# Expert routing one unit earlier on VectorE and ScalarE, in a four-stage attention and mixture-of-experts kernel

## What is computed

```
x = x + tanh(gx[0]) * attention0(layernorm(x), ctx)       # one head of width 128
x = x + tanh(gf[0]) * experts0(layernorm(x))              # 16 experts of width 64, top 4, and a shared one
x = x + tanh(gx[1]) * attention1(layernorm(x), ctx)       # 16 heads of width 8
x = x + tanh(gf[1]) * experts1(layernorm(x))              # 8 experts of width 128, top 2
```

## Time and profile before

| | us |
|---|---|
| median of 3 runs | 331.32 |
| lowest and highest run | 330.4, 331.4 |
| the profiled execution | 328.63 |
| its span, first to last instruction | 326.7 |

### The profile page before, as it was taken

The page is one execution under the profiler, slowest core; times in us unless marked ns, Lnnn a source line. Parts: engine busy times, 40 slices in busy tenths (PEclk is TensorE's granted clock), DMA queues, the critical chain, the costliest instruction groups (busy, mean ns, idle before and its releaser), DMA issues.

```text
span 326.7 us, 5592 instructions
## 1 busy us (share of the span) xinstructions
PE 289.0 (88%) x1470; PEld 216.5 (66%) x1470; DVE 243.6 (75%) x714; ACT 163.1 (50%) x435; POOL 103.4 (32%) x160
## 2 busy tenths in 40 slices
PE   6699699989899599589888888988978999999995
PEld 5588476666566376268778778778856667676662
DVE  2887989689579976546697787877968877868572
ACT  1587542432422232676887887889742242332321
POOL 6374200101191510564549539629110010100000
PEclk9999999999979899959999999999999999999999
DMA  6900175586791420000000000000032242151550
GB/s 220 325 25 0 48 225 156 159 231 192 220 246 48 140 98 32 0 2 0 0 4 0 2 1 0 0 0 3 0 108 99 55 155 104 52 178 33 182 174 32
DMA packets 16408, 28.98 MB, mean 89 GB/s; under 512 B 2661, under 2 KB 4659, under 8 KB 16179
## 3 DMA queue, kind: packets, MB, share of 16 engines
q1 hardware_dynamic: 14312, 27.71, 27.6%
q10 hardware_dynamic: 2072, 0.99, 1.2%
HBM read 24.29 MB, written 1.25 MB: 78 GB/s over the span
## 4 chain that ended last, share of the span: by engine, by line
PE 59%; DVE 15%; ACT 9%; DMA 7%; issue 6%; SPq 4%; DVEq 1%; ACTq 0%
PE bank L564 23%; PE Ybank L586 14%; PE bank L757 4%; DMA CR<-comb_rows 3%; ACT PX L1025 3%; DVE cmx L1410 2%; DMA comb_rows<-ct 2%; PE Tb L503 2%; SPq L326 2%; DMA X<-in_x 2%; DVE recT L1426 2%; ACT QS L1013 1%; PE bank L741 1%; PE bank L602 1%; DVE st L1117 1%
## 5 line engine op out<-in xcount | busy, mean ns | idle before, releaser
L908 ACT ACTIVATE sg<-bank 128x512 f32<-128x512 f32 x64 | 38.0, 595 | 73.7 <-PE bank L564 62.0
L1277 DVE TENSOR_TENSOR hb<-sg,CR 128x512 f32<-128x512 f32 x64 | 44.6, 696 | 17.0 <-issue 7.0
L355 POOL TENSOR_TENSOR rstd<-ve,mhalf 128x4 f32<-128x4 f32 x11 | 11.1, 1011 | 131.5 <-DVE ve L1124 131.5
L1270 DVE TENSOR_TENSOR sg<-sg,bank 128x512 f32<-128x512 f32 x64 | 43.5, 680 | 4.5 <-ACT sg L908 2.2
L1410 DVE TENSOR_REDUCE cmx<-bank 128x4 f32<-128x308 f32 x64 | 28.3, 471 | 17.4 <-PE bank L730 17.2
L564 PE MATMUL bank<-xh,WBH 128*128 128x512 f32 x68 | 35.6, 524 | 5.4 <-DVE sg L1270 4.0
L372 POOL TENSOR_TENSOR KS<-kr,CB 128x1232 fp32r<-128x1232 f32 x16 | 36.2, 2268 | 11.3 <-PE bank L730 11.3
L564 PE MATMUL bank<-xh,UPH 128*128 128x512 f32 x64 | 36.2, 565 | 0.0
L586 PE MATMUL Ybank<-hb,W2T 128*128 128x512 f32 x64 | 33.8, 610 | 1.6 <-DVE hb L1277 1.6
L586 PE MATMUL Ybank<-hb,downw 128*128 128x512 f32 x64 | 32.9, 598 | 0.1
L1025 ACT ACTIVATE PX<-bank,cmx 128x77 f32<-128x77 f32 x128 | 29.3, 354 | 0.0
(11 more groups left out here) (184 smaller groups left out, 598.5 us busy)
## 6 DMA issues: line engine op xcount, KB each, us to landing
CR<-comb_rows SPq DMA_DIRECT2D x64, 128.0 KB, 3.2
CR<-comb_rows SPq DMA_DIRECT2D x32, 256.0 KB, 3.4
VX<-in_vs_seed SPq DMA_DIRECT2D x4, 320.0 KB, 5.5
kr<-kh SPq DMA_DIRECT2D x8, 154.0 KB, 3.2
kr<-kl SPq DMA_DIRECT2D x8, 154.0 KB, 3.3
w13raw<-in_w SPq DMA_DIRECT2D x1, 1088.0 KB, 11.4
X<-in_x SPq DMA_DIRECT2D x4, 256.0 KB, 6.5
upraw<-in_up SPq DMA_DIRECT2D x4, 256.0 KB, 4.5
```

The costliest lines, as they stand in the source:

```text
L355: nc.gpsimd.tensor_tensor(rstd[:], ve[:], mhalf[:], ALU.pow).then_inc(rstd_rdy, 1)
L908: A(sg[:, k % 2, :], Gb[k % 2][:], ACT.Silu).then_inc(m.s_done, 1)
L1270: V.tensor_tensor(sg[:, k % 2, :], sg[:, k % 2, :], Ub[k % 2][:], ALU.mult).then_inc(m.t2, 1)
L1277: V.tensor_tensor(hb[:, k % 2, :], sg[:, k % 2, :], CR[:, k % RING, :], ALU.mult).then_inc(m.h_done, 1)
```

## The change

VectorE's `route_pick` goes from unit 4 to unit 3 and `route_weights` from unit 5 to unit 4; ScalarE's `m_route_tanh` goes from unit 5 to unit 4, and `m_route_copy` from unit 6 to unit 5. In both stages, for all six boundaries. TensorE's and the SP queue's programs are as before.

```diff
@@ ScalarE, m_body
                     if nxt is not None and nxt[1] is not None and k == 3:
                         m_route_act(nxt[1], nxt[2])
+                    if nxt is not None and nxt[1] is not None and k == m.units - 4:
+                        m_route_tanh(nxt[1], nxt[2])
                     if nxt is not None and nxt[1] is not None and k == m.units - 3:
-                        m_route_tanh(nxt[1], nxt[2])
-                    if nxt is not None and nxt[1] is not None and k == m.units - 2:
                         m_route_copy(nxt[1], nxt[2])
@@ VectorE, m_body
                     if nm is not None and k == 3:
                         route_vals(nm, ng)
                         route_top(nm, ng)
+                        route_pick(nm, ng)
                     if nm is not None and k == 4:
-                        route_pick(nm, ng)
-                    if nm is not None and k == 5:
                         route_weights(nm, ng)
                     if stats_of is not None and k == m.units - 2:
                         norm_stats(n + 1, stats_of)
```

## The result

The changed kernel takes 339.12 us (median of 4 runs, 337.77 to 339.48), the kernel before 331.36 beside it (median of 4). The ratio of the runs is 1.0257, with a 95% interval of 1.0207 to 1.0307: slower, by 8.5 us. I had forecast slower, by 4.45 us. Applied to 331.4 us the ratio gives 339.9 us, just above the range that I gave (332.0 to 339.6). The place was right, the size was not. Ratios here are of fast runs alone, and medians of all runs, so a ratio need not be the quotient of two medians; where I set a measurement against a range in microseconds I give both.

The account below looks back on a forecast made before the run. TensorE, busy 88% of the span, was taken as the bound. Six boundary losses summed to +6.15 us, less 1.7 for the clock: +4.45 on the 331.32 us median, giving 335.8 us, range 332.0 to 339.6.

Parts of the forecast that it names:

- the first loss of part 2: Group 1: TensorE, free at 78.92, starts the next group's unit 0 at 79.62, losing 0.70 us.
- "nothing lost" of part 1: VectorE's earlier pick: gating of unit 4 ends at 74.13, before TensorE's 74.30, so nothing is lost.
- the clock's -1.7: Low-clock stretch at 91.1 to 94.5 us goes as TensorE's 1.52 us wait shrinks: -1.7 us, bounds -1.7 to 0.
- The mechanism of part 2: ScalarE's earlier copy waits for TensorE's turn and holds SiLU 6, gating and TensorE: 1.45 us lost at one boundary.
- VectorE's own delay: VectorE's gating of unit 6 starts at 78.88 instead of 77.43, which carries 1.45 us to TensorE's unit 2.
- The boundaries that take up the loss: First stage: TensorE's waits ahead of the logits absorb loss, leaving +0.6 (group 0 to 1) and +0.1 (1 to 2).
- rival B: Late SiLU 6 costs the same, but the clock falls as before: 337.5 us, chance 0.22.
- Rival C: TensorE's new waits lower the clock further, two low stretches of 1.7 us each: 340.9 us, chance 0.1.
- Rival F: The row comes out sooner, removing TensorE's waits of 0.84 and 1.52 us: 329.0 us, chance 0.05.

Follow-up runs that it names:

- copy only: Kernel before with only ScalarE's copy of the turned weights moved one unit earlier, VectorE's program and the tanh unchanged: 336.17 us, ratio 1.0132.
- splits moved: GpSimd's four up-weight splits put behind its first two key expansions: on the kernel before 328.28 us, on the changed kernel 337.44 us.
- both GpSimd moves: Kernel before with GpSimd's splits behind its first two key expansions and the expansions behind VectorE's normalization, routing unchanged: 323.52 us, ratio 0.9840.
- VectorE only: Kernel before with pick, weights and tanh one unit earlier, ScalarE's copy left where it was: 330.99 us, ratio 1.0022.

## Why the prediction was right in place and too small

**ScalarE's wait: right in place, too small.** Three steps of the sum failed: the first loss of part 2, "nothing lost" of part 1, and the clock's -1.7. The mechanism of part 2 is shown by undoing it (no loss in D) and by doing it alone (all of D's loss). The term "TensorE is free at 78.92 and starts at 79.62: 0.70 us lost" was mis-sized. In TensorE's timelines the second product of unit 0 follows the turn's start by 1.20 us before (78.98 less 77.78), by 2.17 after (82.69 less 80.52): 0.97 lost. I had set the six products behind a wait at their usual 1.39. The chain of waits of the changed kernel shows what they take, in D:

```profile
287.82 0.12 PE Tb L616
288.00 0.36 issue
288.56 0.56 ACT sg L908
289.14 0.70 DVE sg L1270
...
292.71 1.65 PE bank L564 x6
294.36 0.86 PE Ybank L586 x2
295.22 1.51 PE bank L564 x6
```

1.65 us: a group of products that starts from a wait has its first weight load open ahead of it, while in the steady run the load goes under the down product. The rows of weight loads agree; the changed kernel first, then before, where the down product runs from 77.89 to 78.91:

```profile
82.35 0.19 PEld L564 LDWEIGHTS bank<-xh,WBH 128*128 128x128 f32 x1 [1.53 <-DVE sg L1270]
```

```profile
78.32 0.19 PEld L564 LDWEIGHTS bank<-xh,WBH 128*128 128x128 f32 x1 [0.24 <-DVE sg L1270]
```

(The Trainium skill, "TensorE: Matmul & The Clock Gate", Step-by-step: what each phase is for, says that weight loads are pulled ahead of running products; the load at 78.32, inside the down product, agrees.) So the first wait of a boundary costs 0.26 more than its idle time. At the last boundary this stays (forecast 0.8, measured 1.21); where VectorE's own delay carries the loss on, as at D's first (1.67 for 1.55), it is swallowed by the next wait.

Part of the rest of D's excess is ScalarE's start. Before, the copy began 0.39 us behind the turn's start at D's second and third boundary (280.62 to 281.01 at the second); after, 0.70 (287.66 to 288.36) and 0.48. All six versions with the copy at unit 5 show 0.69 or 0.70 and 0.47 or 0.48 at the same places, the others 0.39 or 0.40, so it belongs to the order and not to chance. Why the copy starts later there is open.

**VectorE's part: "Nothing lost" was wrong.** I set the end of a gating against the times of TensorE's products in the chain, 74.30 and 76.55. But the timeline of the kernel before has unit 7's first product start at 75.98:

```profile
75.98 0.80 PE L564 MATMUL bank<-xh,WBH 128*128 128x512 f32 x1
```

It overlaps the down product, and its gate must be there by then, 0.6 us sooner than I took it. So what I counted as 0.1 us in group 1 was 0.7: from the logits (72.12) to the copy of the row (80.83) 8.71 us instead of 8.00 (70.08 to 78.08). In group 0 it was 0.3 (9.15 for 8.83). In D the turn came at most 0.1 us later behind the logits than before, as I had said.

**Group 2: the cost of a moved step was taken from another place.** I priced pick and weights by group 1's durations and wrote that they shift nothing. In group 2 the splits of GpSimd run beside the small operations between SBUF tiles, and these take 0.3 to 1.1 us longer than elsewhere. Before, the pick stood behind gating 4, where the splits had ended. Now gating 4 starts 2.7 us later behind the logits (5.54 us, from 95.66 to 101.20, against 2.88) and TensorE waits 2.06 us. Of the 2.7, 1.6 are the pick with its slow copy. The other 1.0 is the two unmoved operations, and copy only has it too (3.90): it comes from where the splits fall against the logits, and why they fell otherwise there is open. I had seen such a clash and used it for the normalization alone. The changed kernel with the splits moved shows it: 8.69 us instead of 10.74. (The Trainium skill, "Advanced Engine Details and Errata", Mode Summary, has VectorE's second SBUF port shared with GpSimd; the trace agrees in that gatings, with one input from PSUM, stay at 0.68 beside a split (at 95.86 in the changed kernel), and goes beyond that section in that a product of two SBUF tiles takes 2.33 us beside a key expansion.)

**The boundaries that take up the loss: mostly right.** Group 1 to 2 gained 0.8 us where I had said 1.6, mostly for the later turn; the wait ahead of the logits and the low clock behind it went as I had said. Group 0 to 1 lost 0.96 for 0.6, by the later turn too.

**The clock's -1.7: there in its stretch, not in the whole.** With the routing of before, the run with the splits moved waited 1.06 us ahead of these logits and the one with both GpSimd moves 0.74, and neither had low clock at 91 us; "VectorE only" waited 1.09 us ahead of the logits at 66.73 and had it there. So the wait of 1.52 us and the low stretch are the profiled execution's, and that the change removed them is not shown. Over the whole kernel nothing came back: the mean granted clock is 0.979 in both profiled executions, and 0.977 to 0.979 in the changed kernel's four runs. That is rival B as far as the clock goes, 337.5 us by my sum without the -1.7; what is left of the way to 339.9 us lies with the two terms above, which are larger still in the traces (4.1 us, below).

**The rivals.** Rival C had the clock fall in the new waits of 0.7 us. It did not: in the changed kernel the granted clock is 1.00 from 17 to 115 and from 255 us on, where all six boundaries with their new waits lie. The rule of the Trainium skill ("TensorE: Matmul & The Clock Gate", A second HAM failure mode) on short idles between groups of matmuls did not bear on gaps of this size in this trace. Rival F, the row sooner out, did not happen in the change, since the turn's place spoke against it; with the turn moved it did, and the two waits that it named went.

Of the 4.7 us between forecast and stretches (9.16 less 4.45, the -1.7 counted in both), the later turns of groups 0, 1 and 2 are 3.1 (0.3 + 0.6 + 2.2; 0.7 of the last copy only has too), the three boundaries of D 1.0 (opened weight load and later copy), and 0.6 in stage B I can't place.

## What to carry to other kernels

A step that waits for another engine should be moved only together with what it waits for: on an engine that works in order the wait now stands ahead of useful work, and here one line on TensorE took back the 2.6% that was lost. When a slack is read from a chain of waits, check it against the start of the overlapping instruction in the timeline, which comes earlier, and add the opened weight load (0.26 us here) to a wait that TensorE gets. Price a moved operation by the engines that run beside it at its new place, and for each group apart. A low-clock stretch behind a wait in one profiled execution may be missing in the next: look for it in several before a forecast counts on it.

## What the runs showed of the hardware

- Products behind a wait: 1.65 us for a group of six that takes 1.39 in a steady run.
- Small VectorE operations between SBUF tiles beside GpSimd's casts and subtractions: 1.28 us for 0.18, 0.81 for 0.18, 0.55 for 0.23. A product of two SBUF tiles of 128x512: 2.33 us for 0.69 beside a key expansion. Gatings with a PSUM input: unchanged.
- ScalarE's start behind the turn's start varied with the place, 0.3 to 0.7 us, in the same way in six versions.
- A wait of TensorE of 1.06 or 1.14 us ahead of the logits was followed by no low clock (splits moved), one of 1.09 us in another version by 3.4 us of it.
